# The first unit's queries, made in the stage before attention

## The reference, cut to what matters

```python
q = _rmsnorm(x @ wq_a.T, q_a_ln_w) @ wq_b.T            # 32 heads of 64 + 64
q_nope, q_pe = (q[..., :NOPE], q[..., NOPE:])
ckv, k_pe = ...                                         # x @ wkv_a.T, 64 + 64
kv = _rmsnorm(ckv, kv_a_ln_w) @ wkv_b.T                 # k_nope 64, v 128 a head
q_pe = _apply_rope(_deinterleave(q_pe), cos, sin)
scores = einsum('bqhd,bkhd->bhqk', q_full, k_full) * softmax_scale   # causal
out = einsum('bhqk,bkhd->bqhd', softmax(scores), v) @ wo.T
```

## Time and profile before

| | us |
|---|---|
| median of three runs | 1950.18 (1947.46 to 1951.13) |
| the profiled execution | 1948.4 |
| its span | 1946.3 |
| TensorE busy | 1814.4 (93%) |
| VectorE busy | 1228.2 (63%) |
| ScalarE busy | 998.1 (51%) |
| GpSimd busy | 870.8 (45%) |

### The profile page before, as it was taken

The page is one execution under the profiler, slowest core; times in us unless marked ns, Lnnn a source line. Parts: engine busy times, 40 slices in busy tenths (PEclk is TensorE's granted clock), DMA queues, the critical chain, the costliest instruction groups (busy, mean ns, idle before and its releaser), DMA issues. The chain is left out here.

```text
span 1946.3 us, 44384 instructions
## 1 busy us (share of the span) xinstructions
PE 1814.4 (93%) x15472; PEld 1425.2 (73%) x15472; DVE 1228.2 (63%) x2653; ACT 998.1 (51%) x2135; POOL 870.8 (45%) x641
## 2 busy tenths in 40 slices
PE   6999969699999999999999999996799999969999
PEld 4678869677777777777777777774588888857887
DVE  5555358388888888988889888895421111125453
ACT  2211047488887878878888788883410100012110
POOL 2232110477877878778787787772000000004321
PEclk9999979899999999999999999998899999989999
DMA  6452152402212122121121221211742233224321
GB/s 225 169 173 87 55 174 93 80 26 72 78 55 83 49 68 78 55 83 56 60 82 55 80 67 49 83 63 56 259 130 87 91 107 104 65 108 169 123 87 66
DMA packets 111695, 182.45 MB, mean 94 GB/s; under 512 B 27472, under 2 KB 64464, under 8 KB 109584
## 3 DMA queue, kind: packets, MB, share of 16 engines
q1 hardware_dynamic: 111632, 181.61, 29.0%
HBM read 122.06 MB, written 59.51 MB: 93 GB/s over the span
## 5 line engine op out<-in xcount | busy, mean ns | idle before, releaser
L942 PE MATMUL psS<-keyT,q 128*128 128x512 f32 (+2 forms) x2304 | 476.0, 352 | 32.2 <-POOL q L1147 24.7
L942 PEld LDWEIGHTS psS<-keyT,q 128*128 128x128 f32 x2304 | 383.3, 190 | 127.0 <-DVE negmax L1073 40.8
L1023 ACT ACTIVATE prob<-prob,negmax 128x640 f32<-128x640 f32 (+7 forms) x512 | 391.9, 767 | 78.3 <-DVE negmax L1073 76.0
L1083 DVE STREAM_TRANSPOSE pT<-prob 128x640 f32<-128x640 f32 (+7 forms) x512 | 380.0, 762 | 65.8 <-PE psV L959 63.2
L1073 DVE CUSTOM_DVE_ANT_0 prob<-psS,mask 128x640 f32<-128x640 f32 (+7 forms) x512 | 371.9, 742 | 40.5 <-PE psS L942 27.1
L413 PE MATMUL f_psy<-f_weff,f_xT 128*128 128x512 f32 x1344 | 314.2, 393 | 0.0
L1309 PE MATMUL o_psy<-o_w,o_o 128*128 128x512 f32 x1344 | 304.8, 389 | 0.0
L1138 POOL TENSOR_TENSOR pT<-pT,cosT 64x512 f32<-64x512 f32 x128 | 164.7, 1286 | 285.2 <-ACT pT L1008 271.1
L1309 PEld LDWEIGHTS o_psy<-o_w,o_o 128*128 128x128 f32 x1344 | 252.3, 188 | 52.4
L413 PEld LDWEIGHTS f_psy<-f_weff,f_xT 128*128 128x128 f32 x1344 | 250.8, 188 | 54.3 <-issue 1.7
L959 PE MATMUL psV<-pT,val 32*64 32x512 f32 (+3 forms) x8192 | 264.9, 407 | 7.1 <-DVE pT L1083 5.9
(11 more groups left out here) (99 smaller groups left out, 1876.1 us busy)
## 6 DMA issues: line engine op xcount, KB each, us to landing
wo<-in_wo SPq DMA_DIRECT2D x16, 1024.0 KB, 5.6
pT<-row_scales SPq DMA_DIRECT2D x128, 128.0 KB, 2.9
oT<-pT SPq DMA_DIRECT2D x64, 256.0 KB, 2.4
o_in<-oT SPq DMA_DIRECT2D x32, 512.0 KB, 5.3
f_xt<-in_x SPq DMA_DIRECT2D x16, 512.0 KB, 4.2
f_w_in<-in_w SPq DMA_DIRECT2D x16, 512.0 KB, 6.2
w_sum<-f_w_in SPq DMA_DIRECT2D x16, 512.0 KB, 5.2
x<-f_xo SPq DMA_DIRECT2D x16, 512.0 KB, 2.7
```

Source lines behind the costliest of these rows:

```text
L942: ins = nc.tensor.matmul(psS[:, slot, start + x0:start + x1], q[:, e, a, t * P:(t + 1) * P], k.keyT[:, m, b * S + x0:b * S + x1], start=(i ...
L1023: nc.scalar.activation(row, row, ACT.Exp, bias=negmax[:, n % 8:n % 8 + 1], scale=-1.0, accum_out=rowsum[:, column(n, s):column(n, s) + 1]) ...
L1083: nc.vector.transpose(pT[:, n % 2, t, 0:width], prob[:, n % RING, 0:width]).then_inc(turned, 1)
```

## The change

A class `Queries` now holds `wn`, `wpe`, `wq`, `q` and the semaphores of folds and queries; both stages use it. In the stage of the latents TensorE makes the first pair's fold at the end of step 2 and the four queries of the first step at the ends of steps 6, 8, 10 and 12, in two banks `psq` that the stage didn't use before. ScalarE splits the folds in step 3, copies the queries at the ends of steps 7, 9, 11 and 13, and makes their high parts at the ends of steps 8, 10, 12 and 14, where it waits for the rotation. VectorE splits the folds in step 3. GpSimd rotates and makes the low parts, behind the mask. `qf` and `swapped` are buffers of the stage. The steps of ScalarE and TensorE are no longer in a loop. In attention the opening fold and the jobs Q, A, H and B of the first step are gone; all else keeps its order.

```diff
+def unrolled(body, steps, lead, lag):
+    for n in range(-lead, steps + lag):
+        body(n, n % 2, lambda m, n=n: 0 <= n + m < steps)
...
+class Queries:
...
+    def products(self, nc, bank, qnT, e, x):
+        for i, (a, m) in enumerate(PASSES):
+            for t in range(QRT):
+                ins = nc.tensor.matmul(bank, self.wq[:, a, e, t, :], qnT[:, m, t, x:x + CHUNK],
+                                       start=(i == 0 and t == 0), stop=(i == 2 and t == QRT - 1))
+        ins.then_inc(self.q_done, 1)
+
+    def copy(self, nc, act, bank, qf, swapped, number):
+        act.wait_ge(self.q_done, number + 1)
+        if later(number, 2):
+            act.wait_ge(self.q_lo, number - 1)
+        nc.scalar.activation(qf, bank, ACT.Copy)
+        nc.scalar.activation(swapped[64:96, :], bank[96:128, :], ACT.Copy)
+        nc.scalar.activation(swapped[96:128, :], bank[64:96, :], ACT.Copy).then_inc(self.q_copied, 1)
...
@@ latents_phase
+        psq = c.ps("psq", [P, 2, BANK])
+        qf, swapped = c.sb("l_qf", [P, 2, CHUNK]), c.sb("l_swapped", [P, 2, CHUNK])
+        queries = k.queries
+        folded_in = 2
+        product_step = {6: 0, 8: 1, 10: 2, 12: 3}
+        copy_step = {step + 1: n for step, n in product_step.items()}
+        high_step = {step + 2: n for step, n in product_step.items()}
...
@@ gpsimd
+            pool.wait_ge(k.tab_in, 48)
+            for n in range(4):
+                if n >= 1:
+                    pool.wait_ge(queries.q_lo, n)
+                x = slice(n // 2 * CHUNK, (n // 2 + 1) * CHUNK)
+                queries.rotate(nc, pool, qf[:, n % 2, :], swapped[:, n % 2, :], k.cosT[64:128, x], k.sinT[64:128, x], n)
+                pool.wait_ge(queries.roped, n + 1)
+                queries.low(nc, pool, qf[:, n % 2, :], n, n)
@@ scalar, at the end of step
+                if n == folded_in + 1:
+                    for e in range(2):
+                        queries.split_fold_hi(nc, act, psq[:, e, :], e, e + 1)
+                if n in copy_step:
+                    m = copy_step[n]
+                    queries.copy(nc, act, psq[:, m % 2, :], qf[:, m % 2, :], swapped[:, m % 2, :], m)
+                if n in high_step:
+                    m = high_step[n]
+                    act.wait_ge(queries.roped, m + 1)
+                    queries.high(nc, qf[:, m % 2, :], m)
-            steady(act, step, NT, 3, 1)
+            unrolled(step, NT, 3, 1)
@@ tensor, at the end of step
+                if n == folded_in:
+                    pe.wait_ge(k.wn_in, 32)
+                    for e in range(2):
+                        queries.fold(nc, psq[:, e, :], e)
+                if n in product_step:
+                    m = product_step[n]
+                    pe.wait_ge(lo2, 4 * (m // 2) + 4)
+                    if m < 2:
+                        pe.wait_ge(queries.f_split, 2)
+                    else:
+                        pe.wait_ge(queries.q_copied, m - 1)
+                    queries.products(nc, psq[:, m % 2, :], k.qnT, m % 2, m // 2 * CHUNK)
-            steady(pe, step, NT, 2, 1)
+            unrolled(step, NT, 2, 1)
@@ vector, at the end of step
+                if not later(n, folded_in + 2) and n == folded_in + 1:
+                    for e in range(2):
+                        queries.split_fold_lo(nc, dve, psq[:, e, :], e, e + 1)
@@ class Round
-                    if not self.absent(job, s) and not (self.first and s < 0) ...
+                    if not self.absent(job, s) and not (self.first and (s < 0 or s == 0 and job in "QHAB")) ...
-            earlier = [("F", 0, -1), ("F", 1, -1)]
+            earlier = [("Q", n, 0) for n in range(4)]
@@ attention_phase, tensor
-            pe.wait_ge(wn_in, 32)
-            for e in range(2):
-                fold_queries(e)
@@ attention_phase, scalar and vector
-            for e in range(2):
-                split_queries_hi(e, e + 1)
-            for e in range(2):
-                split_queries_lo(e, e + 1)
@@ attention_phase, gpsimd
-            pool.wait_ge(tab_in, 48)
```

More of the change, by code:

```diff
@@ L494, in _, with __init__, fold, split_fold_hi @@
             ffn_steps(dve, step)
+class Queries:
+    def __init__(self, c):
+        self.wn = c.sb("wn", [64, 2, QR + KVR])
+        self.wpe = c.sb("wpe", [P, 2, QRT, ROPE])
+        self.wq = c.sb("wq", [P, 2, 2, QRT, QHD], F32R)
+        self.q = c.sb("q", [P, 2, 2, S], F32R)
+        self.f_done, self.f_hi, self.f_split = c.sem("f_done"), c.sem("f_hi"), c.sem("f_split")
+        self.q_done, self.q_copied = c.sem("q_done"), c.sem("q_copied")
+        self.rope_parts, self.roped = c.sem("rope_parts"), c.sem("roped")
+        self.q_hi, self.q_lo = c.sem("q_hi"), c.sem("q_lo")
+    def fold(self, nc, bank, e):
+        for t in range(QRT):
+            ins = nc.tensor.matmul(bank[:, t * NOPE:(t + 1) * NOPE], self.wn[:, e, t * P:(t + 1) * P], self.wn[:, e, QR:QR + KVR],
+                                   start=True, stop=True)
+        ins.then_inc(self.f_done, 1)
+    def split_fold_hi(self, nc, act, bank, e, count):
+        act.wait_ge(self.f_done, count)
+        nc.scalar.activation(self.wq[:, HI, e, :, 0:NOPE], bank[:, 0:QRT * NOPE].rearrange("p (t n) -> p t n", t=QRT), ACT.Copy)
+        nc.scalar.activation(self.wq[:, HI, e, :, NOPE:QHD], self.wpe[:, e, :, :], ACT.Copy).then_inc(self.f_hi, 1)
+    def split_fold_lo(self, nc, dve, bank, e, count):
+        dve.wait_ge(self.f_hi, count)
+        nc.vector.tensor_tensor(self.wq[:, LO, e, :, NOPE:QHD], self.wpe[:, e, :, :], self.wq[:, HI, e, :, NOPE:QHD].bitcast(F32), ALU.subtract)
+        nc.vector.tensor_tensor(self.wq[:, LO, e, :, 0:NOPE], bank[:, 0:QRT * NOPE].rearrange("p (t n) -> p t n", t=QRT),
+                                self.wq[:, HI, e, :, 0:NOPE].bitcast(F32), ALU.subtract).then_inc(self.f_split, 1)
+    def products(self, nc, bank, qnT, e, x):
+        for i, (a, m) in enumerate(PASSES):
+            for t in range(QRT):
+                ins = nc.tensor.matmul(bank, self.wq[:, a, e, t, :], qnT[:, m, t, x:x + CHUNK],
[8 more added lines that the diff above has]
+        nc.scalar.activation(swapped[96:128, :], bank[64:96, :], ACT.Copy).then_inc(self.q_copied, 1)
+    def rotate(self, nc, pool, qf, swapped, cos, sin, number):
+        plain, crossed = qf[64:128, :], swapped[64:128, :]
+        pool.wait_ge(self.q_copied, number + 1)
+        nc.gpsimd.tensor_tensor(plain, plain, cos, ALU.mult).then_inc(self.rope_parts, 1)
+        pool.wait_ge(self.rope_parts, number * 2 + 1)
+        nc.gpsimd.tensor_tensor(crossed, crossed, sin, ALU.mult).then_inc(self.rope_parts, 1)
+        pool.wait_ge(self.rope_parts, number * 2 + 2)
+        nc.gpsimd.tensor_tensor(plain, plain, crossed, ALU.add).then_inc(self.roped, 1)
+    def rows(self, part, n):
+        return self.q[:, n % 2, part, n // 2 * CHUNK:(n // 2 + 1) * CHUNK]
+    def high(self, nc, qf, n):
+        nc.scalar.activation(self.rows(HI, n), qf, ACT.Copy).then_inc(self.q_hi, 1)
+    def low(self, nc, pool, qf, n, number):
+        pool.wait_ge(self.q_hi, number + 1)
+        nc.gpsimd.tensor_tensor(self.rows(LO, n), qf, self.rows(HI, n).bitcast(F32), ALU.subtract).then_inc(self.q_lo, 1)
@@ L737, in jobs @@
                 s = step + shift
-                if not self.absent(job, s) and not (self.first and s < 0) and not (self.last and s > 1) \
+                if not self.absent(job, s) and not (self.first and (s < 0 or s == 0 and job in "QHAB")) and not (self.last and s > 1) \
                         and (shift > 0 or step >= 0) and (shift < 0 or step < 2):
@@ L911, in vacated, with make_queries @@
                         pe.wait_ge(f_split, folds(it, n, s))
[L913 to L919, removed]
+            def make_queries(it, n, s):
                 ch, e, b = n // 2, n % 2, s % 2
                 pe.wait_ge(f_split, folds(it, e, s - s % 2 - 1))
[L923 to L927, removed]
+                queries.products(nc, psV[:, n, :], k.qnT, e, b * S + ch * CHUNK)
             def scores(it, n, s):
@@ L989, in body @@
                             pe.wait_ge(wn_in, (r.it + (s + 1) // 2 + 1) * 32)
-                        fold_queries(n)
+                        queries.fold(nc, psV[:, n, :], n)
             rounds(pe, body)
@@ L1060, in _ @@
         def _(dve):
[L1061 to L1065, removed]
             def maxima(it, n, s):
@@ L1161, in finished @@
                 else:
-                    pool.wait_ge(roped if job == "A" else q_lo, (it * 2 + s) * 4 + n + 1)
+                    pool.wait_ge(queries.roped if job == "A" else q_lo, (it * 2 + s) * 4 + n + 1)
             def body(r):
```

52 lines of the change are left out of this document (14 added, 38 removed).

## The result

The changed kernel takes 1934.38 us (median of six runs, 1932.19 to 1936.82) beside 1949.15 us for the kernel before (six runs, 1947.33 to 1951.13). The ratio is 0.9927, with a 95% interval of 0.9916 to 0.9937, which is 14.2 us less, 12.3 to 16.4 (the two medians by themselves differ by 14.8). Two further series gave 0.9923 [0.9908, 0.9938] and 0.9925 [0.9912, 0.9939].

What follows compares the result with a forecast made beforehand. Attention's head was taken as a chain of latencies, the latents and the rest as bound by TensorE. Gain 20.2 us (16.2 + 4.7 - 0.7) less 7.0 paid is 13.2 off 1950.2: 1937 us, range 1934.5 to 1943.5.

Steps and rivals of the forecast that it cites:

- The opening: Head of attention: queries, keys and banks are ready when the stage opens, so the first score stands 16.2 us earlier.
- From the first score to S10: Head of attention: the score pair starting with S10 comes 11.6 us after the first score, not 16.3; 4.7 us gained.
- VectorE's way to M8: Head of attention: VectorE starts the ninth tile's maximum (M8) 10.7 us after the first score, where it was 13.6.
- GpSimd's chain: Head of attention: the next unit's first copy comes later, putting GpSimd's work nearer the scores needing it; 0.7 us charged.
- The latents: Stage before attention: TensorE pays the moved matmuls in full, 6.6 us, plus 0.4 for ScalarE and VectorE; 7.0 us.
- Rival (a): Stage of the latents goes by ScalarE and GpSimd, so copies and rotation waits are paid: 1942 to 1947 us; chance 0.12.
- Rival (b): VectorE paces the head of attention: only 16.2 us come, 4.7 return as TensorE's waits for maxima: 1941 us; chance 0.09.
- Rival (d): Slower: changed code length makes attention's 14 loop passes show weight-load time; 1955 us at 1.3 us a pass; chance 0.04.

## Why the prediction was right

**The time**: 13.2 us off were forecast and 14.2 measured. The 1937 and the range of 1934.5 to 1943.5 were set against a time before of 1950.2; the measured ratio puts the changed kernel at 1935.9 on that footing, inside. The median as measured, 1934.38, stands beside a time before of 1949.15 and is 0.1 us under the lower end. So the gain was forecast 1 us too small. Its parts were 20.2 gained and 7.0 paid; the traces give 21.6 and 7.1.

**The opening** held to the tenth: the first score stands at the opening, 16.2 us gained; the two queries left in attention (the half move) show that this needs all of the chain moved.

**From the first score to S10** 11.6 us were said and 10.5 measured (11.2 in the second profile, 10.3 in the third). The step was right in kind, M8 and the bank it empties being what S10 waits for (0.68 us <- DVE negmax). The term that was too large is VectorE's way to M8: 9.67 us from the first score for the 10.7 I took. The rows of VectorE between M0 and M8 say why, first of the kernel before, then of the changed one (VectorE's is the third busy time):

```profile
373.70:386.07 12.37, 7.39 (x29) 6.81 (x30) 7.45 (x26) 9.30 (x24) 10.30 (x9) 0.78 0.11 29
```

```profile
365.25:373.75 8.50, 7.67 (x39) 6.81 (x37) 7.19 (x27) 5.22 (x17) 0.00 (x0) 0.87 0.98 219
```

VectorE had 7.45 us of work there before, not 8.8: it was idle 4.9 of the 12.4 us, and I had subtracted 3.6. After, it works 7.19 us and is idle 1.3, where I had left 0.7. The two errors, 1.6 too much and 0.6 too little, make the 1.0. The granted clock has its part in this: it was back at 1.00 by 368 us, 4 us into the head, and I had left all eight tiles at half clock. In the profile where it stayed at 0.50 for 6 us, S10 stood at 11.2, so some 0.7 us of the difference is the clock's. Even there VectorE worked only 7.3 us between M0 and M8 and was idle 1.9, so that 11.6 came within 0.4 by two errors that nearly cancel, which is luck.

**GpSimd's chain**: 0.7 charged, 0.48 us waited (L568).

**The latents**: 7.0 charged, 7.1 measured. TensorE's part is 6.9 for my 6.6, a query costing 1.47 and not 1.37; the trace of the doubled products shows that it is paid in full, the doubled copies that ScalarE's is not. Of the 0.4 charged for ScalarE and VectorE at most 0.2 is left in this profile. That the sum of the stage came out within 0.1 us is partly luck, as a small term too low met one too high, and the stage itself scatters by 0.6 us. Its sign of trouble, TensorE idle before a product in steps 8 to 14, isn't in the trace. The last query was split at 360.1 us, 2 us ahead of the last transposes, as worked out.

**Rival (a)** had a wrong argument against it that happened not to matter. I took from the earlier trace rows that GpSimd doesn't slow VectorE's operations with two operands in SBUF, because 32 of them took 247 to 293 ns "inside a stage where GpSimd is busy". Busy in the stage isn't busy at the moment. GpSimd has a hole there in each pair; one such hole of the kernel before, with the operation in it:

```profile
412.24 2.64 POOL L1147 TENSOR_TENSOR q<-pT,q 128x512 fp32r<-128x512 f32 x2 [0.32 <-ACT q L1015]
...
417.41 0.29 DVE L1063 TENSOR_TENSOR wq<-wpe,wq 128x128 fp32r<-128x128 f32 x1
...
421.83 1.30 POOL L1138 TENSOR_TENSOR pT<-pT,cosT 64x512 f32<-64x512 f32 x1 [6.95 <-ACT pT L1008]
```

The operation at 417.41 stands between 414.88 and 421.83, when GpSimd does nothing. So do the other 31 in the trace: the two of the opening come ahead of GpSimd's first operation there, the rest at least 1.6 us behind the end of its last. In the latents such operations do meet, and the addition waits for the end of GpSimd's operation. The forecast stood because the wait lands on slack: 16 such additions, slowed by half a microsecond on the median, changed nothing that could be measured.

**Rival (b)** had the right engine and too high a price: VectorE does set the head's pace as far as S10, but the head takes 28.15 us, and not the 33.5 (49.7 - 16.2) that the rival needs. **Rival (d)** fell with the straight code alone: same time.

## What to carry to other kernels

Where two stages meet and the second opens with a chain of latencies, find work of that chain whose inputs the first stage already has: here 7.1 us on a saturated engine bought 21.6 us of waiting, and moving half of the chain would have left the second stall in place. Before trusting that another engine's work is free, check slack by its idle share, and check interference by whether the two instructions overlapped in time, not by how busy both were. After such a move look at once for what paces the head; here it is VectorE's maxima and transposes, as far as S10. And when a wait is worked out as span less idle, add up all the idle times of the rows: here 3.6 us were counted of 4.9.

## What the runs showed of the hardware

An operation of VectorE with two tensors in SBUF that started during a GpSimd operation (which read SBUF too) ended 0.08 us after it in all four cases of the changed kernel. It took 0.88 us at the most there instead of 0.21, and up to 1.20 with GpSimd busy throughout, while GpSimd's operation kept its length (1262 to 1311 ns in all 66).

Idle time of about 2.2 and 1.6 us around the last transposes was enough to bring TensorE's granted clock to 0.57 over the next 4 us; with 16 matmuls in those gaps it stayed at 1.00. Of the 1.5 us that the first nine tiles of scores gain by it, all reach the first values, and none could be told in the time. A wait of 4.23 us inside the head brought the granted clock down again, to 0.55 over the next 3.6 us.
